# Phases 4 and 6 of a fused decoder kernel: compact key and query projections expanded by 0/1 products, and one stream of units over all groups

## The reference, cut to what matters

```python
# x, ctx: (16, 128, 128); four cross attentions and four mixtures, each in a gated residual
x = x + tanh(g_xattn[2]) * mha16(layernorm(x), ctx, ctx, mask, Wq, bq, Wk, bk, Wv, bv, Wo, bo)   # phase 4
...
x = x + tanh(g_xattn[3]) * multiscale16(layernorm(x), ctx, ctx, w_q, b_q, ...)                   # phase 6
# both: 16 heads of 8 dimensions
#   Q, K, V = proj(x), proj(ctx), proj(ctx);  softmax(Q K^T / sqrt(8)) V, then the output product
# phase 4: a mask over the keys, the same for all heads and batches
# phase 6: heads 0 to 7 on all 128 positions; heads 8 to 15 on every second position (64 x 64),
#   their outputs interpolated linearly back to 128
```

## Time and profile before

| | |
|---|---|
| runs | 1057.89 us median of 3 (1056.82 to 1060.37) |
| profiled execution | 1052.73 us |
| its span, first to last instruction | 1050.9 us |
| mean granted TensorE clock | 0.933 of 2.4 GHz |
| TensorE busy | 923.4 us (88%) |
| VectorE, ScalarE, GpSimd busy | 550.6, 441.5, 475.1 us |
| phase 4, first product to the end of its last | 453 to 629 us |
| phase 6, the same | 708.5 to 883 us |

### The profile page before, as it was taken

The page is one execution under the profiler, slowest core; times in us unless marked ns, Lnnn a source line. Parts: engine busy times, 40 slices in busy tenths (PEclk is TensorE's granted clock), DMA queues, the critical chain, the costliest instruction groups (busy, mean ns, idle before and its releaser), DMA issues.

```text
span 1050.9 us, 13592 instructions
## 1 busy us (share of the span) xinstructions
PE 923.4 (88%) x4545; PEld 611.1 (58%) x4545; DVE 550.6 (52%) x1536; ACT 441.5 (42%) x782; POOL 475.1 (45%) x441
## 2 busy tenths in 40 slices
PE   5679999975689999989899887667998997999998
PEld 4656666653466666646556554454554564666665
DVE  5534535345454654355765647566556554645632
ACT  2224333244334242236566563334565554343322
POOL 2355567523355746553633513034424422566554
PEclk9689999999789999989999996668999998999999
DMA  7020122040133243200000003000000001342342
GB/s 278 31 81 25 57 81 62 19 135 1 50 113 102 62 142 98 82 1 1 1 1 1 1 4 125 0 1 0 2 1 1 2 1 49 115 130 80 117 125 78
DMA packets 32293, 59.28 MB, mean 56 GB/s; under 512 B 4865, under 2 KB 5249, under 8 KB 32097
## 3 DMA queue, kind: packets, MB, share of 16 engines
q1 hardware_dynamic: 31792, 55.92, 16.7%
q10 hardware_dynamic: 432, 2.50, 0.6%
HBM read 56.90 MB, written 1.51 MB: 56 GB/s over the span
## 4 chain that ended last, share of the span: by engine, by line
PE 76%; DVE 10%; issue 5%; ACT 4%; POOL 2%; DMA 1%; SPq 0%; DVEq 0%; POOLq 0%; ACTq 0%
PE Y L775 16%; PE B L636 8%; PE B L638 8%; PE B L637 8%; PE B L1190 5%; PE B L1125 5%; PE B L1205 4%; PE B L1157 3%; PE B L1164 3%; PE B L1156 2%; PE T L267 1%; ACT shared L1251 1%; PE Y L1220 1%; DMA down_lo<-in_moe 1%; PE T L256 1%
## 5 line engine op out<-in xcount | busy, mean ns | idle before, releaser
L869 POOL TENSOR_TENSOR shared<-shared,bcs 128x512 f32<-128x512 f32 x192 | 244.6, 1279 | 197.3 <-ACT shared L794 140.1
L904 DVE TENSOR_TENSOR shared<-shared,B 128x512 f32<-128x512 f32 x204 | 139.8, 688 | 265.7 <-POOL shared L869 251.3
L794 ACT ACTIVATE shared<-B 128x512 f32<-128x512 f32 x204 | 122.2, 599 | 310.6 <-PE B L638 291.9
L775 PE MATMUL Y<-shared,down_lo 128*128 128x512 f32 x408 | 209.1, 599 | 0.0
L1308 POOL TENSOR_TENSOR shared_r<-shared_r,const 128x512 fp32r<-128x512 f32 (+1 forms) x128 | 126.2, 1018 | 139.0 <-DVE shared_r L1331 105.9
L1377 DVE TENSOR_REDUCE mxh<-B 128x4 fp32r<-128x512 f32 (+1 forms) x128 | 79.2, 620 | 63.8 <-PE B L1157 63.4
L1272 ACT ACTIVATE shared<-B 128x512 f32<-128x512 f32 (+1 forms) x128 | 69.7, 545 | 67.0 <-PE B L1164 66.3
L1644 POOL TENSOR_TENSOR rstd<-var,minus_half 128x4 f32<-128x4 f32 x21 | 21.2, 1010 | 153.0 <-DVE var L234 152.6
L775 PEld LDWEIGHTS Y<-shared,down_lo 128*128 128x128 f32 x408 | 74.5, 191 | 19.1 <-issue 5.7
L636 PE MATMUL B<-shared_r,gate_hi 128*128 128x512 f32 x102 | 81.5, 799 | 0.0
L636 PE MATMUL B<-x_lo,gate_hi 128*128 128x512 f32 x102 | 77.5, 760 | 0.4 <-DVE x_lo L690 0.4
(11 more groups left out here) (278 smaller groups left out, 1711.4 us busy)
## 6 DMA issues: line engine op xcount, KB each, us to landing
bcs<-wrow SPq DMA_DIRECT2D x96, 256.0 KB, 3.4
bcs<-wrow SPq DMA_DIRECT2D x128, 128.0 KB, 3.0
small<-in_small ACTq DMA_DIRECT2D x1, 2406.5 KB, 9.7
gate_lo<-in_moe SPq DMA_DIRECT2D x4, 288.0 KB, 2.9
up_lo<-in_moe SPq DMA_DIRECT2D x4, 288.0 KB, 3.2
down_lo<-in_moe SPq DMA_DIRECT2D x4, 288.0 KB, 3.6
gate_lo<-in_moe SPq DMA_DIRECT2D x4, 272.0 KB, 2.7
up_lo<-in_moe SPq DMA_DIRECT2D x4, 272.0 KB, 3.0
```

The lines of the kernel that those rows point to most:

```text
L775: nc.tensor.matmul(Y[:], w_raw[2][:, at:at + P], hid[c % HIDDEN], start=(i == 0), stop=(i == NC - 1))\
L794: nc.scalar.activation(sg[n % WEIGHTED], B[n % GATES][:], ACT.Silu).then_inc(sem("sg_ready"), 1)
L869: gp.tensor_tensor(sgw[n % WEIGHTED], sg[n % WEIGHTED], bcs[(PLACE.k0[p] + r // m["PER"]) % BROADCAST], ALU.mult)\
L904: nc.vector.tensor_tensor(hid[n % HIDDEN], part, up[:], ALU.mult).then_inc(sem("hh_ready"), 1)
```

## The change

Key and query projections of a group are computed once, 128 wide (`compact`); ScalarE rounds the result to a high part and VectorE takes the low part. A constant 0/1 matrix `sel_r` (loaded as `in_sel`, copied once by VectorE) then spreads 32 rows, the four heads of a quad, to a 128-row tile by two fp32r products (`expand`): high part, then low part. Key tiles are copied by VectorE, query tiles by ScalarE. All of this but the first group's goes through one bank, PJ = B[5], at most one step per unit.

The loop over groups is gone: unit n runs over 4 x 16 units; projections of group g + 1 lie at t = 2 to 13 of group g, its last quad at t = 0 and 1 of group g + 1, and the end of group g at t = 0 to 10 of group g + 1. Weighed sums use one bank (B[4]). The mask is multiplied by the float32r matrix that also serves the shift instead of a bf16 identity. Values have two buffers, `vh` and `vc`. Keys of the next group are multiplied by GpSimd as soon as a buffer is free. The other phases keep their code.

```diff
-        for x in range(NT):
-            tile(0, NG * p, 0, x)
...
+        SC, PT, PV, PJ = B[0:2], B[2:4], B[4], B[5]
+            def compact(g, kq, bank):
+                if kq == "q":
+                    pe.wait_ge(sem("xhat_t_ready"), s0 + g + 1)
+                mm(bank[:], S(f"W{kq}{p}"), context(g) if kq == "k" else xhat_t[g % 2][:], start=True, stop=True)\
+                    .then_inc(sem(f"compact_mm{p}"), 1)
+            def expand(g, kq, a, bank):
+                pe.wait_ge(sem(f"compact_lo{p}"), 2 * g + (1 if kq == "k" else 2))
+                rows = slice(32 * a, 32 * (a + 1))
+                k = 0 if kq == "q" else 2
+                mm(bank[:], sel_r[rows, k * P:(k + 1) * P], comp_hi[kq][rows, :], start=True, stop=False)
+                mm(bank[:], sel_r[rows, (k + 1) * P:(k + 2) * P], comp_lo[kq][rows, :], start=False, stop=True)\
+                    .then_inc(sem(f"{kq}x_mm{p}"), 1)
...
-                        if p == 4:
-                            mm(bank[:], identb, maskb[:].rearrange("p a k -> p (a k)"), start=True, stop=False)
+                if p == 4:
+                    mm(out, minus_r[:], mask_r[:].unsqueeze(1).to_broadcast([P, HEAD_TILES, P]), start=True, stop=False)
...
+            def projections(g, t):
+                if t == 0:
+                    pe.wait_ge(sem(f"qh_ready{p}"), QUADS * g + 3)
+                    expand(g, "k", 3, PJ)
+                elif t == 1:
+                    pe.wait_ge(sem(f"kh_ready{p}"), QUADS * g + 4)
+                    expand(g, "q", 3, PJ)
+                elif g + 1 == NG:
+                    return
+                elif t == 2:
+                    pe.wait_ge(sem(f"qh_ready{p}"), QUADS * g + 4)
+                    compact(g + 1, "k", PJ)
+                elif t == 4:
...
+                    compact(g + 1, "q", PJ)
+                elif t == 6:
...
+                    values(g + 1, PJ)
+                elif t in (8, 10, 12):
...
+                    expand(g + 1, "k", a, PJ)
+                elif t in (9, 11, 13):
...
+                    expand(g + 1, "q", a, PJ)
+            for n in range(NALL + 9):
+                g, t = divmod(n, NU)
+                if n < NALL:
+                    score(n)
+                if 0 <= n - 1 < NALL:
+                    shift(n - 1)
+                if g < NG:
+                    projections(g, t)
+                    if t == 0:
+                        next_rows(g)
+                if g > 0 and t == 6 and p == 6:
+                    upsample(g - 1)
+                if g > 0 and t == 7:
+                    heads_turned(g - 1)
+                if g > 0 and t == 8:
+                    output(g - 1)
+                if g < NG and t == 10:
+                    result(g)
...
+                if 0 <= n - 2 < NALL:
+                    turn(n - 2)
+                if 0 <= n - 3 < NALL:
+                    weigh(n - 3)
+                for q in (n // GB - 2, n // GB - 3):
+                    if 0 <= q < QUADS * NG and ob_at(q) == n:
+                        back(q)
...
+        def heads_act(act, p):
+            for n in range(NALL + 9):
+                g, t = divmod(n, NU)
+                if g < NG:
+                    if t == 0:
+                        norm_act(act, s0 + g + 1, (g + 1) % 2)
+                    if t == 1:
+                        query(g, 3, PJ)
+                    if g + 1 < NG:
+                        if t == 2:
+                            high(g + 1, "k", PJ)
+                        if t == 4:
+                            high(g + 1, "q", PJ)
+                        if t in (9, 11, 13):
+                            query(g + 1, (t - 9) // 2, PJ)
...
+                    nc.scalar.activation(es[n % 2][0:w, 0:4 * w], SC[n % 2][0:w, 0:4 * w], ACT.Exp,
+                                         scale=SCALEH).then_inc(sem(f"es_ready{p}"), 1)
...
+        def heads_pool(pool, p):
+            each(0, 0)
+            power(s0 + 1)
+            each(0, 1)
+            for g in range(NG):
+                each(g, 2)
+                each(g, 3)
+                if g + 1 < NG:
+                    power(s0 + g + 2)
+                    each(g + 1, 0)
+                    each(g + 1, 1)
...
+        def heads_dve(dve, st, p):
+            norm_stats(st, 1)
+            low(0, "k", B[0])
+            low(0, "q", B[1])
+            key(0, 0, B[2])
+            values(0, B[4])
+            key(0, 1, B[5])
+            key(0, 2, B[3])
+            apply(s0 + 1, range(GB))
+            for n in range(NALL + 8):
...
+                if p == 6:
+                    if n == NALL - 8:
                         x_low_dve(dve, 7)
+                    if n == NALL:
+                        pieces = route_dve(dve, st, 7)
+                    next(pieces, None)
...
-            act.dma_start(constb[:], constb_d).then_inc(sem("constb_loaded"), 16)
+            act.dma_start(sel_stage, sel_d).then_inc(sem("sel_loaded"), 16)
...
-            st.add(nc.vector.memset(vh[:], 0.0))
-            st.add(nc.vector.memset(vc[:], 0.0))
-            st.settle()
+            for h in range(2):
+                st.add(nc.vector.memset(vh[h][:], 0.0))
+                st.add(nc.vector.memset(vc[h][:], 0.0))
+            st.settle()
```

More of the change, by code:

```diff
@@ L1128, in values @@
-            def values(g):
-                for j in range(GB):
-                    ins = mm(B[4][:, j * P:(j + 1) * P], context(g, j), S(f"Wv{p}"),
-                             start=True, stop=True)
-                if p == 6:
-                    rows, at, _ = SMALL_AT["Wv6"]
-                    for j in range(GB):
-                        ins = mm(B[5][0:HALF, j * HALF:(j + 1) * HALF], context(g, j, 2),
-                                 small[:, at + HALF:at + P], start=True, stop=True)
-                ins.then_inc(sem(f"v_mm{p}"), 1)
@@ new lines, in values @@
+            def values(g, bank):
+                if p == 4:
+                    for j in range(GB):
+                        ins = mm(bank[:, j * P:(j + 1) * P], context(g, j), S("Wv4"), start=True, stop=True)
+                else:
+                    for j in range(GB):
+                        mm(bank[:, j * HALF:(j + 1) * HALF], context(g, j), S("Wv6", 0, HALF), start=True, stop=True)
+                    for j in range(GB):
+                        c = 2 * P + j * HALF
+                        ins = mm(bank[0:HALF, c:c + HALF], context(g, j, 2), S("Wv6", HALF, P), start=True, stop=True)
+                ins.then_inc(sem(f"v_mm{p}"), 1)
@@ new lines, in weigh @@
+            def weigh(u):
+                g, a, j, w = unit(p, u)
+                q = QUADS * g + a
+                pe.wait_ge(sem(f"pt_ready{p}"), u + 1)
+                if u % NU == 0:
+                    pe.wait_ge(sem(f"v_ready{p}"), g + 1)
+                if j == 0 and q > 0:
+                    pe.wait_ge(sem(f"os_ready{p}"), q)
+                heads = P // w
+                for i in range(0, HEAD_TILES, heads):
+                    if coarse(p, a):
+                        val = vc[g % 2][:, j * (HEADS // 4) + 2 * (a - 2) + i // 2, :]
+                    else:
+                        val = vh[g % 2][:, j * HEADS + 4 * a + i, :]
+                    ins = mm(PV[VW * i:VW * (i + heads), j * w:(j + 1) * w], val,
+                             pt[u % 2][:, i // heads * w:(i // heads + 1) * w], start=True, stop=True)
+                ins.then_inc(sem(f"pv_mm{p}"), 1)
@@ new lines, in upsample @@
+            def upsample(g):
+                pe.wait_ge(sem(f"osb_ready{p}"), QUADS * (g + 1))
+                if g + 1 < NG:
+                    pe.wait_ge(sem("xhat_t_ready"), s0 + g + 3)
+                else:
+                    pe.wait_ge(sem("logits_read"), PLACE.no[7] + 1)
+                for y in range(2):
+                    ins = mm(T[:, y * P:(y + 1) * P], K("up")[:, y * P:(y + 1) * P],
+                             oc[:].rearrange("p x n d -> p (x n d)"), start=True, stop=True)
+                ins.then_inc(sem("up_mm"), 1)
@@ L1396, in build @@
+            for _ in pieces:
+                pass
         area5 = Area()
@@ L1669, in _ @@
                     continue
[L1670 to L1674 removed]
+                heads_pool(pool, p)
         @block.scalar
@@ L1762, in packed, with selection @@
     return out
[L1765 to L1770 removed]
+def selection():
+    out = np.zeros((HEADS // HEAD_TILES, HEAD_TILES, DK, 4, HEAD_TILES, 4, DK), np.float32)
+    for copy in range(4):
+        for i in range(HEAD_TILES):
+            for d in range(DK):
+                out[:, i, d, 0 if copy < 2 else 1, i, copy, d] = 1.0
+                out[:, i, d, 2 if copy % 2 == 0 else 3, i, copy, d] = 1.0
+    return out.reshape(P, 4 * P)
 def constants():
```

538 lines of the change are left out of this document (257 added, 281 removed).

## The result

The changed kernel takes 1066.15 us (median of 20 runs, 1051.12 to 1072.07), the kernel before 1056.27 (20 runs, 1049.62 to 1063.05). The ratio is 1.0067, 95% interval 1.0037 to 1.0096: slower, by 7 us, where 12.9 were to be won. The profiled run took 1065.07 us, its span is 1063.2.

A forecast was written before the change was run, and what follows sets the result against it. TensorE, busy over nine tenths at full clock, was taken as the bound. Start +3.0, openings -3.0 -3.0, cycles -6.0 -12.0, last groups +3.8 +1.8 +.5, meeting extras +2.0: -12.9, giving 1045 us, range 1029 to 1058.

The forecast's parts named there:

- Cycle of phase 6: One group of phase 6: 39.55 us less 5.0 waiting, plus .5 and .5, gives 35.55, 4.0 less.
- Cycle of phase 4: One group of phase 4: 41.65 us less 4.6 waiting, plus .5, 1.6 and .5, gives 39.65, 2.0 less.
- the mask's .10: Phase 4's mask product: the fp32r stationary side loads slower than bf16, +.10 us a unit, 1.6 a group.
- meeting extras: Units where two or three extras meet (t=10, t=16): waits of .25 us a group, +2.0 over 8 groups.
- Row switch: Each expansion on TensorE: going to fewer rows and back costs .27 us a pair, making .72 per expansion.
- Rival (c): An expansion's second half can't load during its first: 50 x .19 = 9.5 us later, 1054; chance .10.
- Last groups: Each phase's last group also carries its predecessor's end: +3.8 us in phase 4, +1.8 in phase 6.
- Openings: Opening of phases 4 and 6: first maximum earlier, 3 us less in each, bounds 1 and 5.
- Start: VectorE clears a second vh and vc before the first statistics: +3.0 us, bounds 0 and 3.1.
- Tail: Drain behind phase 6's last unit: one more routing piece on VectorE's queue ahead of the last division, +.5 us.
- (b): Expansions cost only what they stream, 13.5 us less, giving 1031; chance .22.
- (d): Projection steps through the single bank stall TensorE: gain gone at .16 us more each, 1077 at .4; chance .10.

The follow-up runs named there:

- e3_openings_start: Changed kernel, but GpSimd's opening key multiplies wait for VectorE's normalization, and GpSimd clears the second vh and vc at the start: 1049.09 us, ratio .9925 to before.
- e4_bf16_mask: Changed kernel with phase 4's mask product back on the bf16 identity and bf16 mask: 1060.15 us, ratio 1.0052 to before.
- e9_narrow_phase4: Changed kernel with each phase 4 expansion's first 32-row product issued five times instead of once: 1081.86 us, ratio 1.0233 to before.
- e6: e1_all_rows with a tiny, overwritten 32-row product before each expansion, so the row changes return: 1048.77 us, ratio .9934 to the kernel before.
- e1_all_rows: Changed kernel with expansions reading all 128 rows through zero-padded 0/1 matrices, in both phases: 1034.89 us, ratio .9813 to before.
- e8_combined: Changed kernel with expansions over all rows, both edits of e3_openings_start, and the bf16 mask in phase 4: 1021.94 us, ratio .9683 to before.
- e5_64_rows: e1_all_rows with each expansion reading 64 rows, its quad's 32 and 32 zero ones: 1048.13 us, ratio .9920 to the kernel before.
- e13: Changed kernel with one more, overwritten product over all 128 rows before each expansion of phase 6: 1067.43 us, ratio 1.0161 to before.
- e14: As e13, but the added product reads only the quad's 32 rows: 1082.53 us, ratio 1.0305 to the kernel before.

## Why the prediction was wrong, step by step

- **Cycle of phase 6, the step that failed.** Forecast 35.55, measured 42.17 (with the opening's slow stretch), 42.87, 44.44. The prediction gave every product its duration at the full clock, because phase 6 of before had it, and asked of the clock only whether it rises earlier in the openings. At the full clock the step was right: e3_openings_start took 36.11 with .7 us of slow-clock loss in it (.98), so 35.4. The three cycles and the last group cost 14.1 more than before where 10.2 less were forecast; these 24.3 us are nearly the whole error of 25.2 between the two profiled runs (12.3 against -12.9). What the runs showed in its place: with 32-row expansions among the coarse units TensorE stands at half clock for 19 and 24 us of a cycle (1.4 and 12.9 where the same instructions fell least), with 64 rows for none, and then the kernel takes 1048.1 against 1056.6, a gain of 8.5.
- **Cycle of phase 4.** Forecast 39.65, measured 40.15. That it is so near is partly luck, since terms were off both ways. An expansion costs .82, not .72: 8 x .10 = .8. The waits were set too high, .24 in all instead of .5 and .25. The bare unit is at 1.66 to 1.67, as forecast, and e4_bf16_mask shows that the mask's .10 is its price there, but over the cycle it is .91, not 1.6. These three come to -.4, so with the .25 for meeting extras counted (39.9) about .65 of the cycle isn't placed.
- **Row switch.** Forecast .27 a pair from the coarse shifts, measured .35 (.82 - .47). It has a part that no row of before showed: the second half stands .33 behind the first, .10 more than it streams. Rival (c) had .40 and .19 for that. It isn't a load that can never hide: in e9_narrow_phase4 further narrow products follow each other at .232, the second half of the expansion among them, and only the one right behind the change of rows is late. "TensorE: Matmul & The Clock Gate" of the Trainium skill, Part 3, would have both halves apart in either form; the 128-row halves, .24 apart, disagree with it. The price comes with a change of rows. "TensorEngine Tiling (Array Packing)" of the Trainium skill, Key Properties, says that a change of the tiling mode drains the engine; the .31 before the first half and the .39 of the e6 run agree with it, and the .10 between the halves it doesn't cover.
- **Last groups.** Phase 4: first to last score 26.42 to 30.65, +4.2 (forecast +3.8). Phase 6: 24.31 to 27.7 in e1_all_rows, +3.4 (forecast +1.8), and 30.30 with its own falls. The kernel before has 3.4 us at half clock in each of these two stretches, the changed kernel none in phase 4's and e1_all_rows none in phase 6's, so at equal clock both terms were 1.7 larger still.
- **Openings.** Forecast: first maximum 11 us behind the phase's first product. Measured 13.3 (458.48 to 471.75; 14.1 before, 452.99 to 467.09) in phase 4 and 14.9 in phase 6. The chain was right, one term in it not: the normalization was taken at 1.1, and beside GpSimd's multiplications it takes 4.05. With GpSimd kept away (e8_combined) it is 10.2 and 11.6. In the sum: -.8 and -2.1 instead of -3.0 twice.
- **Start.** Forecast +3.0, measured +3.6 (first statistics 8.99 against 5.38): the small memsets count too. Up to phase 4's first product it is 5.5; the other 1.9, in phases 0 to 3 and the setup, aren't placed, and against them the stretch with phase 5 is 1.2 shorter. Both are over the 1 us that the prediction allowed the other phases, with opposite signs.

```profile
4.61 1.76 DVE L1862 MEMSET vh<- 128x2048 f32 x1 [0.38 <-issue]
...
8.99 0.87 DVE L224 BATCH_NORM_STATS2 stats<-X 128x6 f32<-128x128 f32 x4
```

- **Tail.** Forecast +.5, measured +2.3 (13.95 to 16.29 from the last score to phase 7's first product). VectorE's in-order queue is the cause, as named, but it stands idle 3.82 for ScalarE's sigmoid before the routing piece, and the division that TensorE wants is behind both:

```profile
883.67 0.29 DVE L561 TENSOR_TENSOR s<-sig,small 128x128 f32<-128x128 f32 x1 [3.82 <-ACT sig L665]
...
885.18 0.22 DVE L1473 TENSOR_TENSOR shared<-Y,rden 128x64 f32<-128x64 f32 x1
```

```profile
885.55 0.66 PE L1202 MATMUL Y<-const,shared 128*128 128x128 f32 x2 [3.12 <-DVE shared L1473]
```

- **Rivals.** (b), expansions at what they stream, was put at 1031; e1_all_rows, where they do, takes 1034.9, but it takes all rows to get there. (d), the single bank, cost next to nothing: TensorE's waits for the copies of query tiles, from phase 4's second group to phase 6's end, sum to .6 us, the longest .2, and those for key tiles to .8, all in phase 6's opening. The rival that came true, a loss of clock in the steady groups, wasn't among them.

## What to carry to other kernels

When products over few rows are added to a stretch whose products are small already, look at the granted clock as the first term of the sum: here 32 rows instead of 64, with the same columns, cost 1.5% (1.0067 against .9920). Selecting rows with zeros in a full-height 0/1 matrix costs memory and .8 us once (the copy of `sel_r` in the setup takes 1.22 instead of .42), nothing in each product, and it spares the change of rows too. And when work moves next to other work, take durations from rows where the neighbour engine is busy as it will be.

## What the runs showed of the hardware

The granted clock falls to .78 with TensorE busy 42.34 of 42.87 us, and stays at 1.00 in e5_64_rows with 33.96 of 35.03. "TensorE: Matmul & The Clock Gate" of the Trainium skill, Part 1, describes the gate by how busy the engine has been; these windows show that busy time as the profile counts it doesn't settle it. The rows that products work on count, as e5_64_rows, e6_switch_only and the pair e13/e14 show, even where the added rows hold zeros. They don't count alone, as e9_narrow_phase4 shows (1.00 with six 32-row products in a unit).

VectorE's four normalizations go in step with GpSimd's four multiplications: 4.05 us instead of 1.11, to the end of GpSimd's 4.03. "SBUF — State Buffer" of the Trainium skill, section "Who interferes with whom", says that a VectorE instruction in a two-port mode and GpSimd share a pair of ports and that one of them blocks fully. The two rows above fit that; the mode of the VectorE instruction isn't in the trace.

Going to 32 rows and back costs .35 us a pair, in three places: .10 before the first narrow product, .09 between it and the second, and .16 behind them (.10 up to the transposes, .06 in them). 64 rows cost the same as 32 (unit 2.48 in both).
